# A mixture of experts joined to the cross attention's program

## What is computed

```python
x = x + cross_attention(layernorm(x), context, mask, Wq, Wk, Wv, Wo)
h = layernorm(x)
sc = einsum('bth,sh->bts', h, Wr)                  # 32 experts
_, idx = top_k(sc, 2)
m = one_hot(idx, 32).sum(axis=-2)
g = softmax(sc) * m
g = g / (g.sum(-1, keepdims=True) + 1e-8)
hU = einsum('bth,shr->btsr', h, U)                 # rank 16
out = einsum('bts,btsr,srh->bth', g, hU, V)
aw = sigmoid(attr @ Wa[0])
x = x + out * (0.9 + 0.2 * (g @ aw)[..., None])
```

## Time and profile before

| | us |
|---|---|
| three runs | 2543.62, 2545.8, 2546.73 |
| the profiled execution, its own time | 2545.78 |
| its span, first to last instruction | 2543.8 |
| PE busy | 2398.7 (94%) |
| DVE busy | 1731.7 (68%) |
| ACT busy | 1188.6 (47%) |
| GpSimd busy | 156.3 (6%) |

### The profile page before, as it was taken

One profiled execution on the slowest core, in us unless ns is written; L12 is line 12 of the kernel. 1 busy time (PEld: TensorE's weight loads), 2 busy tenths in 40 slices (PEclk: granted clock), 3 DMA queues, 4 the chain that ended last, 5 costly groups with the idle time before them and its releaser, 6 DMA issues. The chain is left out here.

```text
span 2543.8 us, 38038 instructions
## 1 busy us (share of the span) xinstructions
PE 2398.7 (94%) x11280; PEld 1766.3 (69%) x11280; DVE 1731.7 (68%) x3680; ACT 1188.6 (47%) x2330; POOL 156.3 (6%) x263
## 2 busy tenths in 40 slices
PE   7899998799999899999989999999999999998779
PEld 6555556577777688655557777777777777776457
DVE  6577877778877664667656666666667666666643
ACT  3477756333333432577745444444444444444321
POOL 0000000100000000000030010101010000100100
PEclk9999999899999999999999999999999999999789
DMA  5622201000000135433211000000000000000101
GB/s 167 194 71 72 75 25 43 1 1 0 0 0 1 54 126 165 132 97 92 72 35 66 5 17 4 16 4 16 4 16 11 9 12 8 12 0 0 43 1 66
DMA packets 71914, 110.40 MB, mean 43 GB/s; under 512 B 14266, under 2 KB 25274, under 8 KB 71194
## 3 DMA queue, kind: packets, MB, share of 16 engines
q1 hardware_dynamic: 71834, 109.38, 14.2%
HBM read 75.26 MB, written 34.08 MB: 43 GB/s over the span
## 5 line engine op out<-in xcount | busy, mean ns | idle before, releaser
L3159 DVE SCALAR_TENSOR_TENSOR x_res<-xa_out_bank,xa_den,x_res 128x512 f32 (+1 forms) x256 | 191.4, 748 | 157.9 <-PE xa_out_bank L2706 157.9
L3030 ACT ACTIVATE xa_pT_hi<-xa_t_bank 128x512 fp32r<-128x512 f32 x256 | 149.5, 597 | 125.5 <-PE xa_t_bank L2874 125.5
L501 DVE TENSOR_REDUCE l1s_mx<-l1s_max_bank 128x1 f32<-128x512 f32 x256 | 156.5, 682 | 68.8 <-PE l1s_max_bank L359 68.7
L3041 ACT ACTIVATE xa_prob<-xa_prob,xa_nmax 128x512 f32<-128x512 f32 x256 | 182.7, 716 | 29.7 <-DVE xa_nmax L3126 29.7
L2706 PE MATMUL xa_out_bank<-xa_o_w,xa_o_hi 128*128 128x512 f32 x512 | 173.4, 420 | 22.4 <-DVE x_res L3159 20.7
L3108 DVE TENSOR_TENSOR xa_pT_lo<-xa_t_bank,xa_pT_hi 128x512 fp32r<-128x512 f32 x256 | 175.7, 687 | 22.0 <-ACT xa_pT_hi L3030 17.9
L501 DVE TENSOR_REDUCE l0s_mx<-l0s_max_bank 128x1 f32<-128x512 f32 x256 | 156.7, 682 | 46.3 <-PE l0s_max_bank L359 46.2
L3126 DVE CUSTOM_DVE_ANT_0 xa_prob<-xa_s_bank,xa_mask_bias 128x512 f32<-128x512 f32 x256 | 171.1, 687 | 22.7 <-PE xa_s_bank L2706 11.2
L2166 DVE SCALAR_TENSOR_TENSOR ffn_yT<-ffn_y,ffn_ysc,ffn_yT 128x512 f32<-128x512 f32 x176 | 129.6, 746 | 46.8 <-PE ffn_y L1912 46.7
L2874 PE MATMUL xa_t_bank<-ident,xa_prob 128*128 128x128 f32 x1024 | 150.0, 274 | 0.1
L2874 PEld LDWEIGHTS xa_t_bank<-ident,xa_prob 128*128 128x128 f32 x1024 | 120.2, 140 | 39.7 <-issue 18.3
(11 more groups left out here) (475 smaller groups left out, 5794.5 us busy)
## 6 DMA issues: line engine op xcount, KB each, us to landing
l0s_q<-l_q SPq DMA_DIRECT2D x96, 128.0 KB, 2.4
l1s_q<-l_q SPq DMA_DIRECT2D x96, 128.0 KB, 3.0
l1s_k<-l_k SPq DMA_DIRECT2D x96, 128.0 KB, 3.2
l0s_k<-l_k SPq DMA_DIRECT2D x96, 64.0 KB, 2.4
x_res<-in_x_dram SPq DMA_DIRECT2D x4, 1024.0 KB, 9.9
l_q<-l_q_hi SPq DMA_DIRECT2D x16, 256.0 KB, 2.6
l_q<-l_q_lo SPq DMA_DIRECT2D x16, 256.0 KB, 3.2
l_q<-l_hi SPq DMA_DIRECT2D x16, 256.0 KB, 2.1
```

Of the source, the lines that this page charges most:

```text
L501: dve.tensor_reduce(self.mx[:, j // QT, j % QT:j % QT + 1], self.max_bank[j % 3][:], AX.X, ALU.max)\
L3030: act.activation(pT_hi[:, kt % (QT - 1), :], t_bank[kt % 2][:], ACT.Copy).then_inc(pT_hi_done, 1)
L3041: act.activation(prob[:, q, :], prob[:, q, :], ACT.Exp, bias=nmax[:, q:q + 1], scale=-1.0, accum_out=den[:, r, 0, q:q + 1]).then_inc(exp_d ...
L3159: dve.scalar_tensor_tensor(xt, out_bank[:], den[:, r, 2, q:q + 1], xt, ALU.mult, ALU.add)\
```

## The change

The mixture is no longer a stage. `cross_attention` and `routed_mixture` only collect arguments and build one program, `attend_and_mix`; a class `Mixture` issues the mixture's instructions inside it. `norm_to_features`, `Preparation`, `norm_stats` and `keep_turning` are gone, and with them one stage change, the barrier inside the mixture and the idle matmuls. What is done where:

- SP loads the five weights as soon as the last vT is projected. Their tiles lie where the context, masks and other tiles of the cross attention lay, and several tiles of the mixture lie on one another.
- GpSimd clears, makes the masks, and splits V (high parts by a copy, low parts by a subtraction, `rest_values`), which ACT and DVE did before. It waits for scores, turnings and weighings of the last unit.
- The last three units are written out. In unit 30, DVE takes the statistics of batches 0 and 1. In unit 31, PE turns Wr (one job instead of four), U (four jobs) and x tiles 0 to 5 through a `Ring` of two banks, ACT makes high parts and normalises (DVE did that before, from SBUF), and DVE makes low parts, the statistics of batch 2 and the attributes' product.
- After unit 31, `Mixture.tensor`, `scalar` and `vector` give a fixed order in which the last projections, x tiles 6 to 15, the scores, the choice by batches of 4 tiles (operations on 128x128), the gates and the first hidden groups are interleaved. Three roots now stand on ACT between exponentials.
- The loop over batches 1 to 3 is written out; the arithmetic of each step is as before.

The diff, cut to the order of the three engines after unit 31, to the functions that the prediction speaks of, and to unit 31 on PE (its second head) and DVE:

```diff
+class Mixture:
+
+
+    def __init__(self, st, Wr, U, V, attr, Wa, out):
...
+    def normalise(self, act, t):
+        act.wait_ge(self.scales_ready, 1 if t < 2 * QT else t // QT)
+        if t >= QT:
+            act.wait_ge(self.ring.turned, self.XX + t - QT + 1)
+        act.activation(self.xn[t % QT], self.st.x[:, t, :], ACT.Identity, bias=self.norm.mv[:, 4, t:t + 1],
+                       scale=self.norm.mv[:, 3, t:t + 1]).then_inc(self.norm.xn_ready, 1)
...
+    def copy_hidden(self, act, i):
+        act.wait_ge(self.hu_done, i + 1)
+        if i == 0:
+            act.wait_ge(self.v_lo_done, self.FC)
+        reached(act, self.z_made, i - 1)
+        act.activation(self.hu[i % 2], self.hu_bank[i % 2][:], ACT.Copy).then_inc(self.hu_copied, 1)
...
+    def tensor(self, pe, project_out, added):
+        project_out(0)
+        self.turn_x(pe, 6)
+        project_out(1)
+        self.turn_x(pe, 7)
+        self.score(pe, 0)
+        project_out(2)
+        self.turn_scores(pe, 0)
+        self.turn_x(pe, 8)
+        project_out(3)
+        self.turn_x(pe, 9)
+        self.score(pe, 1)
+        self.turn_x(pe, 10)
+        self.turn_x(pe, 11)
+        self.turn_scores(pe, 1)
+        self.hidden(pe, 0, 0)
+        self.score(pe, 2)
+        self.turn_scores(pe, 2)
+        self.turn_gates(pe, 0)
+        self.hidden(pe, 0, 1)
+        self.turn_x(pe, 12)
+        self.turn_x(pe, 13)
+        self.spread_weights(pe, 0, 0)
+        self.turn_x(pe, 14)
+        self.turn_x(pe, 15)
+        self.hidden(pe, 0, 2)
+        pe.wait_ge(added[0], added[1])
+        self.spread_weights(pe, 0, 1)
+        self.score(pe, 3)
+        self.hidden(pe, 0, 3)
+        self.turn_scores(pe, 3)
+        self.spread_weights(pe, 0, 2)
+        self.turn_gates(pe, 1)
+        self.spread_weights(pe, 0, 3)
+        for b in range(1, B):
+            for c in range(self.FC):
+                self.hidden(pe, b, c)
+                self.spread_weights(pe, b, c)
+                self.mix(pe, b - 1, c)
+                if c == 1 and b + 1 < B:
+                    self.turn_gates(pe, b + 1)
+        for q in range(QT):
+            self.mix(pe, B - 1, q)
...
+    def scalar(self, act):
+        self.norm.root(act, 1, batch_tiles(2))
+        self.take_x_hi(act, 6)
+        self.take_x_hi(act, 7)
+        act.wait_ge(self.aw_in, 1)
+        act.activation(self.aw[:, 1, :], self.aw[:, 0, :], ACT.Exp, scale=-1.0).then_inc(self.aw_out, 1)
+        self.copy_scores(act, 0)
+        self.normalise(act, 8)
+        self.normalise(act, 9)
+        self.take_x_hi(act, 8)
+        self.normalise(act, 10)
+        self.normalise(act, 11)
+        self.take_x_hi(act, 9)
+        self.copy_scores(act, 1)
+        self.take_x_hi(act, 10)
+        self.take_x_hi(act, 11)
+        self.exponential(act, 0)
+        self.norm.root(act, 2, batch_tiles(3))
+        self.copy_hidden(act, 0)
+        self.copy_scores(act, 2)
+        self.normalise(act, 12)
+        self.normalise(act, 13)
+        self.take_gates_hi(act, 0)
+        self.copy_hidden(act, 1)
+        self.normalise(act, 14)
+        self.normalise(act, 15)
+        for t in range(12, T):
+            self.take_x_hi(act, t)
+        self.take_z_hi(act, 0)
+        self.copy_hidden(act, 2)
+        self.exponential(act, 1)
+        self.take_z_hi(act, 1)
+        self.copy_scores(act, 3)
+        self.copy_hidden(act, 3)
+        self.take_z_hi(act, 2)
+        self.exponential(act, 2)
+        self.take_gates_hi(act, 1)
+        self.take_z_hi(act, 3)
+        for i in range(self.FC, B * self.FC):
+            self.copy_hidden(act, i)
+            if i == self.FC + 1:
+                self.exponential(act, 3)
+            self.take_z_hi(act, i)
+            if i % self.FC == 1 and i < (B - 1) * self.FC:
+                self.take_gates_hi(act, i // self.FC + 1)
...
+    def choose(self, dve, b):
+        sc, e, g, top, idx, idx_f = self.sc[b % 2], self.e, self.g[b % 2], self.top, self.idx, self.idx_f
+        full = [P, QT, self.NS]
+        numbers = self.number[:].to_broadcast(full)
+        dve.wait_ge(self.sc_taken, b + 1)
+        for q in range(QT):
+            last = dve.max(top[:, q, :], sc[:, q, :])
+        self.link(dve, last)
+        for q in range(QT):
+            last = dve.max_index(idx[:, q, :], top[:, q, :], sc[:, q, :])
+        self.link(dve, last)
+        dve.tensor_tensor(e[:], sc[:], top[:, :, 0:1].to_broadcast(full), ALU.subtract).then_inc(self.e_in, 1)
+        self.link(dve, dve.tensor_copy(idx_f[:], idx[:, :, 0:2]))
+        dve.wait_ge(self.e_in, b + 1)
+        dve.wait_ge(self.made, 1)
+        reached(dve, self.g_turned, b - 1)
+        self.link(dve, dve.tensor_tensor(sc[:], numbers, idx_f[:, :, 0:1].to_broadcast(full), ALU.is_equal))
+        self.link(dve, dve.tensor_tensor(g[:], numbers, idx_f[:, :, 1:2].to_broadcast(full), ALU.is_equal))
+        self.link(dve, dve.tensor_tensor(g[:], g[:], sc[:], ALU.add))
...
+    def vector(self, dve, add_attended):
+        self.scales(dve, 1)
+        add_attended(0)
+        self.norm.tile_stats(dve, 12)
+        self.take_x_lo(dve, 6)
+        add_attended(1)
+        self.norm.tile_stats(dve, 13)
+        self.take_x_lo(dve, 7)
+        add_attended(2)
+        self.norm.tile_stats(dve, 14)
+        self.take_scores(dve, 0)
+        self.take_x_lo(dve, 8)
+        add_attended(3)
+        self.norm.tile_stats(dve, 15)
+        self.take_x_lo(dve, 9)
+        self.norm.combine(dve, 2, batch_tiles(3))
+        self.choose(dve, 0)
+        self.take_x_lo(dve, 10)
+        self.take_x_lo(dve, 11)
+        self.take_scores(dve, 1)
+        self.finish_attributes(dve)
+        self.scales(dve, 2)
+        self.gate(dve, 0)
+        self.choose(dve, 1)
+        self.take_scores(dve, 2)
+        self.take_gates_lo(dve, 0)
+        self.take_x_lo(dve, 12)
+        self.take_x_lo(dve, 13)
+        self.weigh_hidden(dve, 0)
+        self.take_x_lo(dve, 14)
+        self.take_x_lo(dve, 15)
+        self.take_z_lo(dve, 0)
+        self.weigh_hidden(dve, 1)
+        self.take_z_lo(dve, 1)
+        self.gate(dve, 1)
+        self.take_scores(dve, 3)
+        self.weigh_hidden(dve, 2)
+        self.take_z_lo(dve, 2)
+        self.choose(dve, 2)
+        self.take_gates_lo(dve, 1)
+        self.weigh_hidden(dve, 3)
+        self.take_z_lo(dve, 3)
+        self.gate(dve, 2)
+        for b in range(1, B):
+            for c in range(self.FC):
+                i = b * self.FC + c
+                self.weigh_hidden(dve, i)
+                self.take_z_lo(dve, i)
+                self.add(dve, b - 1, c)
+                if b == 1 and c == 0:
+                    self.choose(dve, 3)
+                if b == 1 and c == 2:
+                    self.gate(dve, 3)
+                if c == 1 and b + 1 < B:
+                    self.take_gates_lo(dve, b + 1)
+        for q in range(QT):
+            self.add(dve, B - 1, q)
...
+                pool.wait_ge(mixture.v_in, 16)
+                pool.wait_ge(scored, units_q * NU)
+                for c in range(mixture.FC):
+                    mixture.split_values(pool, c)
+                pool.wait_ge(turned, units_q * NU)
+                for c in range(3):
+                    mixture.rest_values(pool, c)
+                pool.wait_ge(weighed, NR * NU)
+                mixture.rest_values(pool, 3)
...
                         else:
                             next_q(0)
                             out(0)
+                            if is_last(u):
+                                mixture.turn_weights(pe, mixture.UU + 3)
                             next_q(1)
                             out(1)
+                            if is_last(u):
+                                mixture.turn_x(pe, 0)
                             next_q(2)
                             if not is_last(u):
                                 turn_v(u + 1)
                             out(2)
+                            if is_last(u):
+                                mixture.turn_x(pe, 1)
                             turn_probabilities(u, r, 0)
                             turn_probabilities(u, r, 1)
+                            if is_last(u):
+                                mixture.turn_x(pe, 2)
                             out(3)
+                            if is_last(u):
+                                mixture.turn_x(pe, 3)
                             turn_probabilities(u, r, 2)
                             weigh(u, s, r, 0)
                             turn_probabilities(u, r, 3)
...
                         if is_first(n):
                             add_last(0)
                         invert_sum(n, r)
+                        if is_last(u) and r == 1:
+                            mixture.norm.tile_stats(dve, 8)
+                            mixture.norm.tile_stats(dve, 9)
+                            mixture.take_weights_lo(dve, mixture.UU + 3)
                         add_last(1)
+                        if before_last(u):
```

(49 more changed lines are left out.)

758 lines of the change are left out of this document (347 added, 411 removed).

## The result

The changed kernel takes 2505.9 us, the median of 4 runs (2505.2 to 2508.9), against 2544.7 (2541.9 to 2546.7) for the kernel before on the same chip: ratio 0.985, 95% interval 0.9838 to 0.9862. The profiled execution has a span of 2503.6 us; before it was 2543.8. The forecast was 2512, range 2498 to 2530.

The account below looks back on a forecast made before the run. PE, busy 94%, bounds the kernel, so only the program's end can gain. A walk of the PE, ACT and DVE queues takes 191.6 us to 146.4 (-45.2); with +1.5, +1 and +9, -33.7: 2512 us, range 2498 to 2530.

Parts of the forecast that it names:

- Parts 1 and 5: Last unit's first head: ring turnings, low parts and a late weighing, +1.4 us; statistics and combine on DVE, +1.5 us.
- Part 2: Last unit's second head: inserts on DVE delay the maxima and the add freeing the out bank, +10.4 us.
- Part 3: Last weighing to batch 1's first hidden group: 36.7 us of PE work plus 10.3 of stalls, 47.0 us.
- Part 4: Loop over three batches: 83.4 us plus 4.2 of waits at its start, 87.6 us; the tail stays 6.3.
- Part 5: Weight loads and GpSimd's masks, clears and V split are hidden and cost nothing; statistics and combine on DVE +1.5 us.
- Part 6: ACT: six table switches instead of two, 5.1 us more, where ACT would wait anyway; taken as 0.
- Part 7: GpSimd's V low parts may hold up DVE's combine of batch 2: bounds 0 to 5.5 us, taken as 1.
- Part 8: PE's clock falls to 1.2 GHz in the second head and again around turn_gates(0): 9 us taken.
- that the clock holds and nothing collides: Rival for the program's end: no clock fall, no GpSimd collision, -45 to -47 us, 2500 us; chance 0.15.
- That the clock stays at 1.2 GHz until the loop: Rival: recurring stalls keep PE at 1.2 GHz up to the loop, -12 to -17 us, 2529 to 2534; chance 0.12.
- that it does so in the loop: Rival: PE stays at 1.2 GHz in the loop as well, slower, 2595 us, or 2554 with half doubled; chance 0.03.
- That it does not overlap: Rival: moved work only lengthens last unit and chain, small choice operations costing 0.69 instead of 0.29, -19 us, 2526; chance 0.1.

Follow-up runs that it names:

- the kernel with the combine moved: Changed kernel with the six small DVE instructions combining batches 0 and 1 moved from unit 30's end to behind unit 31's first-head second row addition: 2507.3 us.
- The attributes' experiment: Changed kernel with the attributes' product and its sum on DVE moved into unit 31's first head, behind the second row addition: 2508.2 us.
- The seven-edit kernel: Changed kernel with DVE and ACT reordered: attributes' product, batch 2's scores, U's parts, combine, tile statistics, first row addition, tiles 14 and 15: 2492.7 us.
- the control: The changed kernel itself, unaltered, run once more beside the last-unit and gate experiments: 2508.7 us, ratio 0.9862 to the kernel before.
- the run with extra matmuls: Changed kernel with 16 unused matmuls before the last head's second projection and 9 before turn_gates(0), filling PE's waits: 2510.2 us.
- one overlap taken away: Changed kernel with PE made to wait for batch 0's gates before its first hidden group: 2516.5 us.

## Why the prediction was right

Point by point, between the cuts of the windows above.

- **Parts 1 and 5, first head: +2.9 forecast, +4.4 measured.** The combine ahead of the maxima costs 1.3 us of the 1.5 that were taken for it and the statistics (the wait 2.29 against 1.01, and 1.00 once it is moved). What was missing is the clock: I had no fall of it in this head. It stood at 0.90, and at 1.00 in the kernel with the combine moved, whose head is 2.7 us shorter, 1.3 us of wait and 1.4 of clock.
- **Part 2, second head: +10.4 forecast, +11.7 measured.** Forecast were 5.1 us of wait at the second projection and 3.2 at the third; it was 4.6 and 2.0, both at the named queue. Between o_lo and the first maximum the walk says 6.3 us (its terms add up to 6.05), and 6.1 were measured. The attributes' experiment shows the mechanism. The size is partly luck: with the weighings and ring turnings the walk had 11.3 us of waits, the profile has 7.2 in waits of over 0.35, and PE was busy 16.8 us at clock 0.72 where the walk had 11.0 of work.
- **Part 3: 47.0 forecast, 53.4 measured.** Of its stalls the second projection (2.8 forecast, 2.5 measured), turn_gates(0) (2.7, 2.8) and tile 14 (2.3, 2.1) came as walked, and each went with its own edit. The seven-edit kernel takes 42.9 for this part at clock 1.00; with the 5.6 us of waits that its edits took out here, the changed kernel would take 48.5. By this difference my walk was 1.5 short, and 4.9 are the clock (3.0 in the control). PE's busy time says the same: 44.8 us here, 43.0 in the control, 40.0 with seven edits.
- **Part 4, loop 87.6 forecast, 87.2 measured;** the tail 6.9 for 6.3. Here too errors cancel: the waits at its start are 1.1 and 1.25 us, not 4.2, and PE was busy 84.8 us, not 83.4. In the control one group of twelve at the loop's start took 4.6 instead of 3.0 us, again the clock, and its loop 88.8.
- **Part 5, what hides the loads and GpSimd.** No wait of PE of over 0.35 us in the end part is put down to a DMA or to GpSimd. GpSimd ended at 2359.14, and the copy of hidden(0,0), the first that needs V's parts, started at 2378.68. The statistics in unit 30 cost nothing that shows: from the start of `l1s_score_bank` to the cut are 1283.6 us before and 1283.7 now.
- **Part 6, table loads at nothing.** Six loads, as forecast:

```profile
2318.13 0.19 ACT L3134 ACTIVATION_READ_ACCUMULATOR xa_prob<-xa_prob,xa_nmax 128x1 f32 x1
2318.33 1.28 ACT L493 ACT_TABLE_LOAD   x1
2319.62 0.21 ACT L493 ACTIVATE mixn_mv<-mixn_mv 128x8 f32<-128x8 f32 x1
```

 One follows the other within 0.02 us. By the Trainium skill (ScalarE: Activation LUTs, What ACT_TABLE_LOAD costs) a drain of about 1380 ns belongs to each switch; in this trace there is none on either side of the load.
- **Part 7, GpSimd against DVE: +1 forecast, nothing measured,** because the two hardly met:

```profile
2354.12 5.02 POOL L2270 TENSOR_TENSOR mix_room<-mix_v,mix_room 128x512 fp32r<-128x512 f32 x4 [12.27 <-PE xa_t_bank L2945]
```

```profile
2358.97 0.19 DVE L483 TENSOR_TENSOR mixn_mv<-mixn_bn 128x4 f32<-128x4 f32 x1
2359.20 0.17 DVE L484 TENSOR_TENSOR mixn_mv<-mixn_bn 128x4 f32<-128x4 f32 x1
```

 GpSimd ended at 2359.14, 0.17 us into the first operation of the combine. That one took 0.19 us, and 0.15 in the control, where GpSimd was done 0.6 us before it. So the price of a longer collision was neither confirmed nor refuted here.
- **Part 8, the clock: +9 taken, 6 to 7 measured.** 1.4 in the first head, in the second nothing up to the third projection by the run with extra matmuls and perhaps 0.5 behind it, 4.9 up to the loop. This term was mis-sized and partly misplaced: I put one of its two falls into the second head, where it counts little, and none into the first. The walk's own misses, 1.3 us in the second head (with the clock's 0.5), 1.5 in part 3 and 0.6 in the tail, fill the gap, so that -33.7 stands beside -34.8 partly by errors that cancel.

The forecast number is 6 us high all the same, 1 us by the end part and 5 by the execution: the changed kernel's profile happened to reach the last unit 5.4 us sooner than the one of before, and had gained that before the first row of `l1s_score_bank`. Which stage ahead of that does it is open.

Of the rivals, that the clock holds and nothing collides fell with the windows (0.90, 0.72, 0.90), though nothing collided. That the clock stays at 1.2 GHz until the loop is refuted by the same windows, and that it does so in the loop by 1.00 there. That it does not overlap is refuted twice: with one overlap taken away the time is 7.9 us longer, and an operation of the choice on 128x128 takes 0.29 us and the next starts 0.32 later, as I took it, not 0.69:

```profile
2375.95 0.29 DVE L2541 TENSOR_TENSOR mix_sc<-mix_number,mix_idx_f 128x128 f32<-128x128 f32 x1
2376.27 0.29 DVE L2542 TENSOR_TENSOR mix_g<-mix_number,mix_idx_f 128x128 f32<-128x128 f32 x1
```

None of the signs of being wrong appeared: the second head took 24.1 us, turn_gates(0) waited 2.8, and the loop waits only at its start.

## What to carry to other kernels

When work is woven into a stage that PE dominated, look at what each insert stands ahead of on the other engines: one addition that frees a bank, put off by 5.4 us by inserts and the wait for one of them, made PE wait 4.6 us. The changed kernel left 16 us on the table that reordering alone won. And when runs scatter by more than the effect, cut the profiles at a common event and compare from there.
